# Two output projections of a graph and attention block, from one f32 matmul to three f32r matmuls

## The reference, cut to what matters

```
# layer 0, inside the mixing branch
out = transpose(out).reshape(B, N, DIM)
x = xn + (out @ proj_w + proj_b)              # xn: the normalised input of the branch
h = layernorm(x, ln2_g, ln2_b)                # goes to the MLP; x + xn rows are kept for the sum
# layer 1: the same product with W_proj, b_proj; the branch's result is
gamma * layernorm_core(xn + out @ W_proj + b_proj) + beta
```

## Time and profile before

| what | value |
|---|---|
| median of three runs | 3432.07 us (3430.57 to 3433.05) |
| profiled execution | 3428.94 us, of which the span is 3427.2 us |
| mean granted TensorE clock | 0.933 |
| PE busy | 2888.5 us, 84% of the span |
| DVE busy | 2312.9 us, 67% |
| ACT busy | 1449.7 us, 42% |
| GpSimd busy | 462.6 us, 13% |
| `proj0` (first load issued to next stage's first load) | 702.25 to 820.02 us |
| `proj1` (first load issued to next stage's first load) | 2771.16 to 2882.87 us |

### The profile page before, as it was taken

One profiled execution on the slowest core, in us unless ns is written; L12 is line 12 of the kernel. 1 busy time (PEld: TensorE's weight loads), 2 busy tenths in 40 slices (PEclk: granted clock), 3 DMA queues, 4 the chain that ended last, 5 costly groups with the idle time before them and its releaser, 6 DMA issues. The chain is left out here.

```text
span 3427.2 us, 50208 instructions
## 1 busy us (share of the span) xinstructions
PE 2888.5 (84%) x17656; PEld 2481.1 (72%) x17656; DVE 2312.9 (67%) x4167; ACT 1449.7 (42%) x2424; POOL 462.6 (13%) x327
## 2 busy tenths in 40 slices
PE   1999996967999998887988599868999977887794
PEld 1999995745788998777986233248999955777794
DVE  4665652735851553998664888657788858998775
ACT  3464552213112332555243577521546512554345
POOL 2287885200000000000002310000000000000000
PEclk9999998988999999999999699979999988999997
DMA  8333325694211653623131311253311077212301
GB/s 249 85 49 57 47 33 134 213 220 98 77 44 56 184 174 98 170 66 80 35 75 29 98 40 45 55 167 120 72 46 45 23 178 212 76 50 78 84 21 47
DMA packets 255535, 319.45 MB, mean 93 GB/s; under 512 B 97933, under 2 KB 179342, under 8 KB 255208
## 3 DMA queue, kind: packets, MB, share of 16 engines
q1 hardware_dynamic: 177576, 272.11, 29.4%
q0 software_dynamic: 77760, 44.83, 6.6%
HBM read 236.35 MB, written 79.53 MB: 92 GB/s over the span
## 5 line engine op out<-in xcount | busy, mean ns | idle before, releaser
L195 POOL DMA_INDIRECT adj_d<-edge_val,edge_off x160 | 332.5, 2078 | 184.6 <-DVE edge_off L183 100.0
L3191 DVE TENSOR_TENSOR expert_wgel<-expert_gel,expert_wps 128x417 f32<-128x417 f32 (+1 forms) x384 | 203.0, 584 | 57.0 <-PE expert_wps L3116 46.6
L2102 PE MATMUL gat00att_ops<-gat00att_h,gat00att_p 125*125 x1600 | 198.2, 280 | 48.4 <-DVE gat00att_p L2076 48.4
L2102 PE MATMUL gat10att_ops<-gat10att_h,gat10att_p 125*125 x1600 | 195.9, 279 | 48.4 <-DVE gat10att_p L2076 48.4
L2102 PEld LDWEIGHTS gat00att_ops<-gat00att_h,gat00att_p 125*125 125x125 f32 x1600 | 183.8, 189 | 63.0 <-issue 63.0
L2102 PEld LDWEIGHTS gat10att_ops<-gat10att_h,gat10att_p 125*125 125x125 f32 x1600 | 184.1, 192 | 60.8 <-issue 60.8
L3163 ACT ACTIVATE expert_gel<-expert_hps 128x417 f32<-128x417 f32 (+1 forms) x384 | 193.5, 519 | 64.2 <-DVE expert_wgel L3191 52.5
L577 PE MATMUL perf_wide<-y_lo,perf_qk_hi 128*128 128x416 f32 (+1 forms) x432 | 154.9, 359 | 24.7 <-DVE perf_qk_lo L759 24.4
L1275 PE MATMUL fc_ps<-y_lo,fc_w_hi 128*128 128x512 f32 (+1 forms) x432 | 154.6, 358 | 22.3 <-DVE fc_w_lo L1317 22.3
L1428 PE MATMUL fc_ops<-fc_w_hi,fc_x_lo 128*125 128x384 f32 x480 | 163.7, 341 | 7.1 <-DVE fc_w_lo L1480 7.1
L715 ACT ACTIVATE perf_kphi<-perf_wide,perf_lnm 125x384 f32<-125x384 f32 (+1 forms) x180 | 95.7, 630 | 172.5 <-PE perf_wide L601 171.6
(11 more groups left out here) (491 smaller groups left out, 7932.0 us busy)
## 6 DMA issues: line engine op xcount, KB each, us to landing
fc_w<-in_L_mix_fc_w SPq DMA_DIRECT2D x96, 384.0 KB
adj_d<-edge_zero POOLq DMA_DIRECT2D x22, 546.9 KB
gat00proj_adj<-adj_d POOLq DMA_DIRECT2D x20, 546.9 KB, 7.0
perf_keys<-keys_d SPq DMA_DIRECT2D x20, 437.5 KB
gat00att_sh<-shift_d SPq DMA_DIRECT2D x16, 546.9 KB
sh<-shift_d SPq DMA_DIRECT2D x16, 546.9 KB
perf_w<-in_L_mix_qkv_w SPq DMA_DIRECT2D x18, 384.0 KB
perf_w<-in_L_mix_W_qkv SPq DMA_DIRECT2D x18, 384.0 KB
```

The costliest lines, as they stand in the source:

```text
L195: edges.nc.gpsimd.indirect_dma_start(out=edges.adj_flat[u].rearrange("(n a) -> n a", a=1), out_offset=bass.IndirectOffsetOnAxis(ap=edges.o ...
L2102: ins = pe.matmul(ops[0:TP, u, b, t * w:(t + 1) * w], p[:, s, (t0 + t) * TP:(t0 + t + 1) * TP], h[:, s, bass.ds(hd, 1), :], start=(s == 0 ...
L3191: dve.tensor_tensor(wgel[:, q % W, 0:cn], gel[:, q % 3, 0:cn], wps[:, q % 3, 0:cn], ALU.mult).then_inc(wgel_done, 1)
```

## The change

Both projections are computed as three f32r matmuls for each f32 one. Weight and turned rows are each split into a high part (the value rounded to f32r) and a low part (what is left): ACT writes the high part, DVE subtracts it and writes the low part. PE then adds `hi x lo`, `lo x hi` and `hi x hi` for every block and half. The other parts of the change:

- `w` is loaded in 6 blocks of rows instead of 2 halves of columns, and `a` tile by tile with a semaphore each. `a` of tile 1 is now issued behind the whole of `w`. All else stays in its order, except that `a` of tiles 5 to 9 are five pairs of transfers.
- `w` lies in the space of `x` tiles 4 to 9 (`xw`), so SP waits until `w` is split before it issues `x` of tiles 2 to 4 and what follows.
- The loop over blocks is outside that over halves.
- The bias add (`base`) moves from DVE to GpSimd, as does in `proj1` the add of the shift rows to `x` (`shift_row`) and the one add of `more`. GpSimd does them in one list, in `proj1` base and shift in turn for each tile.
- `kept` now counts only the split tiles of `a`; the turned results of `proj0` have `y_kept`.

```diff
-        x = S.sb("x", [TP, NT, D])
-        w = S.sb("w", [128, KB, D])
-        aT = S.sb("aT", [128, 2, KB, TP])
+        xw = S.sb("xw", [128, NT, D])
+        x, w = xw[0:TP], xw[:, NT - KB:NT, :]
+        w_hi, w_lo = S.sb("w_hi", [128, KB, D], F32R), S.sb("w_lo", [128, KB, D], F32R)
+        aT_hi, aT_lo = S.sb("aT_hi", [128, 2, KB, TP], F32R), S.sb("aT_lo", [128, 2, KB, TP], F32R)
...
-                load_tiles(a, attn_d, a_ld, 0)
-                load_w(0)
-                load_w(1)
+                load_a(0)
+                for kb in range(KB):
+                    load_w(kb)
+                load_a(1)
                 move_rows(sp, bias[:], row_bcast(bias_d, TP), bias_ld)
...
+                load_tiles(h, xn_d, xn_ld, 1)
+                sp.wait_ge(w_split, KB)
+                load_tiles(x, x_d, x_ld, 1)
+                for t in range(5, NT):
+                    load_a(t)
+                load_tiles(h, xn_d, xn_ld, 2)
+                load_tiles(x, x_d, x_ld, 2)
...
+                    for kb in range(KB):
                         if t == 0:
-                            pe.wait_ge(w_ld[c], 16)
+                            pe.wait_ge(w_split, kb + 1)
+                        for c in range(2):
+                            for n, (ap, wp) in enumerate(((aT_hi, w_lo), (aT_lo, w_hi), (aT_hi, w_hi))):
+                                ins = pe.matmul(hps[0:TP, t % 2, c * 512:c * 512 + half], ap[:, t % 2, kb, :],
+                                                wp[:, kb, c * half:(c + 1) * half], start=(kb == 0 and n == 0),
+                                                stop=(kb == KB - 1 and n == 2))
...
+                    act.copy(aT_hi[:, t % 2], turned_a(t)).then_inc(a_high, 1)
+
+                def high_w(kb):
+                    act.wait_ge(w_ld[kb], 16)
+                    act.copy(w_hi[:, kb, :], w[:, kb, :]).then_inc(w_high, 1)
...
+                def base(t):
+                    if t in first_of:
+                        pool.wait_ge(xn_ld[first_of[t]], 32)
+                    pool.tensor_tensor(h[:, t, :], h[:, t, :], bias[:], ALU.add).then_inc(based, 1)
+                def shift_row(t):
+                    if t in first_of:
+                        pool.wait_ge(x_ld[first_of[t]], 32)
+                    pool.tensor_tensor(x[:, t, :], x[:, t, :], rows[0:TP, 1, :], ALU.add).then_inc(shifted, 1)
...
+                for t in range(2, NT):
+                    base(t)
+                    if not turn:
+                        shift_row(t)
...
+                def low_a(t):
+                    dve.wait_ge(a_high, t + 1)
+                    dve.tensor_tensor(aT_lo[:, t % 2], turned_a(t), aT_hi[:, t % 2].bitcast(F32), ALU.subtract).then_inc(kept, 1)
+
+                def low_w(kb):
+                    dve.wait_ge(w_high, kb + 1)
+                    dve.tensor_tensor(w_lo[:, kb, :], w[:, kb, :], w_hi[:, kb, :].bitcast(F32),
+                                      ALU.subtract).then_inc(w_split, 1)
...
+                low_a(0)
+                for kb in range(KB):
+                    low_w(kb)
                 for t in range(NT):
+                    if t + 1 < NT:
+                        low_a(t + 1)
                     project(t)
```

More of the change, by code:

```diff
@@ L994, in proj_stage @@
     first_of = {t0: p for p, (t0, _) in enumerate(pieces)}
+    half = D // 2
     turns = [("a", 0)]
@@ L1155, in _ @@
                         keep_y(t)
+            @block.gpsimd
+            def _(pool):
+                def base(t):
[6 more added lines that the diff above has]
+                    pool.tensor_tensor(x[:, t, :], x[:, t, :], rows[0:TP, 1, :], ALU.add).then_inc(shifted, 1)
+                pool.wait_ge(bias_ld, 32)
+                base(0)
+                base(1)
+                if not turn:
+                    pool.wait_ge(rows_ld, 96 if more is not None else 64)
+                    if more is not None:
+                        pool.tensor_tensor(rows[0:TP, 1, :], rows[0:TP, 1, :], more[:], ALU.add).then_inc(more_added, 1)
+                        pool.wait_ge(more_added, 1)
+                    shift_row(0)
+                    shift_row(1)
+                for t in range(2, NT):
+                    base(t)
+                    if not turn:
+                        shift_row(t)
             @block.vector
@@ L1163, in _ @@
                     shifts.keep(dve)
-                dve.wait_ge(bias_ld, 32)
+                def low_a(t):
[5 more added lines that the diff above has]
+                                      ALU.subtract).then_inc(w_split, 1)
                 def project(t):
-                    if t in first_of:
-                        dve.wait_ge(xn_ld[first_of[t]], 32)
-                    steps_done.done(dve.tensor_tensor(h[:, t, :], h[:, t, :], bias[:], ALU.add))
+                    dve.wait_ge(based, t + 1)
                     dve.wait_ge(h_done, t + 1)
-                    steps_done.wait()
                     both = h[:, t, :].rearrange("p (c n) -> p c n", c=2)
@@ L1181, in normalise @@
                 def normalise(t):
[L1182 to L1183 removed]
                     if turn:
+                        if t in first_of:
+                            dve.wait_ge(x_ld[first_of[t]], 32)
                         dve.tensor_tensor(x[:, t, :], x[:, t, :], h[:, t, :], ALU.add).then_inc(sum_ready, 1)
@@ L1195, in normalise @@
                         steps_done.done(dve.tensor_tensor(h[:, t, :], h[:, t, :], rows[0:TP, 0, :], ALU.mult))
-                        steps_done.done(dve.tensor_tensor(x[:, t, :], x[:, t, :], rows[0:TP, 1, :], ALU.add))
+                        dve.wait_ge(shifted, t + 1)
                         steps_done.wait()
@@ L1208, in _ @@
                         dve.wait_ge(rows_ld, 96 if more is not None else 64)
-                        if more is not None:
-                            steps_done.done(dve.tensor_tensor(rows[0:TP, 1, :], rows[0:TP, 1, :], more[:], ALU.add))
-                            steps_done.wait()
                     if t:
```

50 lines of the change are left out of this document (25 added, 25 removed).

## The result

Over the runs taken together the kernel before has a median of 3432.97 us (3430.57 to 3436.07, 8 runs) and the changed one 3415.43 (3406.62 to 3422.74, 8 runs): ratio 0.9948, interval 0.9936 to 0.996, so 14 to 22 us faster. The forecast was 3414. The profiled execution took 3415.68 us with a span of 3413.6; before it was 3427.2.

The account below looks back on a forecast made before the run. PE was taken to bound both projections, at 9.03 and 8.38 us a tile. Gains of 13.1 - 2 = 11.1 us in `proj0` and 10.9 - 4 = 6.9 in `proj1`, 18.0 together, gave 3414 from 3432.07; range 3402 to 3427.

Parts of the forecast that it names:

- The products: PE's tiles in both stages: f32r products take 6.96 us a tile in `proj1`, 7.61 in `proj0`, 1.42 less each.
- The head: Start of each stage: first product from 716.8 and 2785.5, second product ending 1.7 and 1.6 us earlier than before.
- later than 720: Sign against the forecast, at the head of `proj0`: a first product starting after 720 would show it wrong.
- The late `x`: GpSimd's list in `proj1`: `x` lands at about 2839, delaying tile 6's bias add and the last product by 5.3 us.
- what the sum had without exclusion: `proj1` before any price for GpSimd's adds: 16.2 us less 5.3 for the wait on `x`, 10.9 us gained.
- the 16.2 of the forecast: `proj1`: gain from PE and DVE taken alone, without the wait on `x` or a price for GpSimd's adds.
- DVE's tail: End of `proj1`: DVE's 9.5 us after the last product lose two shift adds of 0.95 each, leaving 7.6.
- The exclusion: GpSimd's adds beside DVE in both stages: they stop DVE steps, costing 2 us in `proj0` and 4 in `proj1`.
- in full: Rival: GpSimd's adds stop DVE for their whole length, 6 us in `proj0`, 11 in `proj1`; 3425 us; chance 0.20.
- No price: Rival: GpSimd's adds cost DVE nothing in either stage, gains 13.1 + 10.9 = 24.0 us; 3408 us; chance 0.22.
- so the gain is passed on whole: Stages behind start with a barrier and their own loads, so the two stages' 18.0 us shorten the whole kernel.

Follow-up runs that it names:

- e2: The changed kernel with GpSimd's bias and shift adds cut to one column each, order and waits kept: 3401.01 us.
- e9: The changed kernel with all adds back on DVE, `proj1`'s norm fused into two steps, and 101 empty DVE instructions in `proj0`: 3389.25 us.
- e3: The changed kernel with all bias adds of a piece ahead of its shift adds in GpSimd's list: 3414.28 us.
- e8: The changed kernel with 112 empty DVE instructions at the head of `proj0`: 3403.73 us.
- e11: The changed kernel with 40 empty DVE instructions ahead of the first subtraction in `proj0`: 3402.30 us.
- e7: The kernel before with 117 empty DVE instructions at the head of `proj0`: 3417.48 us.
- e12: The changed kernel with only the shift adds back on DVE, bias adds still on GpSimd, and 113 empty DVE instructions: 3403.95 us.

## Why the prediction was right, and where it was not

- **The products** went as said: 6.96 us a tile.
- **The head.** Forecast: first product from 14.5 us after the stage's start in `proj0`, done at 23.4. Measured: 721.11 - 706.6 = 14.5, taken up by DVE at 729.39 - 706.6 = 22.8. In `proj1` DVE took it up at 2784.49, 23.1 after the start, and 23.2 was the forecast. The absolute test ("later than 720") was badly put: the stage began 4.3 us later.
- **The late `x`.** The forecast had it at 2839, 67.8 us after the stage's start; GpSimd took it up 66.7 after. Product 8 waited 3.46 us, at the place named; an earlier wait of 2.49, ahead of product 4, was not named. In `e2`, with the waits and without wide adds, `proj1` gave 10.9 us, just what the sum had without exclusion. But the term was sized at 5.3, and PE's waits for the low part in `e2` add up to 2.9 us. In `e9`, where GpSimd stands idle, the last matmul of the stage begins 87.2 us after its start, in `e2` 90.0, so the late `x` was worth about 3. That puts `proj1` without it at a gain of some 13.7 us (an estimate, 10.9 + 2.8) and not at the 16.2 of the forecast. One part of the difference is DVE's tail up to the next stage's first load, which became 1.3 us shorter and not 1.9. Two errors of some 2.5 us cancelled, and that is luck.
- **The exclusion.** Against the stages of `e2` those of the changed kernel are 1.1 us longer in `proj0` (2 taken) and 5.0 in `proj1` (4 taken); in the other f32r kernels with both sets of adds (`e3`, `e8`, `e11`) it is 6.2 to 6.5 in `proj1`. DVE's blocked steps in `proj1` add up to 14.9 us, as the two groups shown and the tensor_scalar (9.8, 0.68 each alone) give: 17.2 - 9.6 + 12.0 - 7.7 + 9.8 - 6.8. Slack took the larger part, about 10 us. The rival "in full" (11 us) is refuted by the stage's length, though the blocked time is even more than it said. "No price" is refuted by the rows. (The DVE step of 2.92 us in the earlier trace rows, which the forecast calls an add, is a multiplication; it has two SBUF inputs all the same.)
- **Added when they overlap.** In the changed kernel DVE was 0.88 us early for the late bias add, not 3.76 as in `e2`: it had been stopped before. The two terms share their time; that their sum was near is partly chance.
- **The step without a ground** is "so the gain is passed on whole". By the medians it held: 17.5 us against the stages' 17.3. But `e7` shows that the stages outside can move the time by 15 us through DVE's instruction count alone, and no term of the forecast had a place for it. The total came right because the loop stalls at 2182 and at 2187 alike (263.7 and 263.5 us). A begin at 2227, 40 instructions further, gave 13 us more (`e11`).

## What to carry to other kernels

An add moved from DVE to GpSimd is paid for in DVE's steps with two SBUF inputs and in its scalar and cast passes beside it: compare what it frees with what it stops, and try first to fold DVE's own steps. Where a program has a runtime loop of some hundred instructions, as the 294 here, a change of code ahead of it can add or take its stall; look for idle time released by "issue" at the loop's turns, and compare variants at the same place of the loop.

## What had not been expected

- Idle time of 2.6 to 2.9 us at each jump back of a DVE loop, set by where its 294 instructions begin. With the fall of TensorE's clock that follows most of them it is 10 to 11 us in the loop, more than half of this change's whole effect.
- In `proj0` GpSimd's adds stop a cast (2.18 us instead of 0.55) and a tensor_scalar with one SBUF input (2.01 instead of 0.68), but never an add with a PSUM operand (0.96 us at most in all fourteen traces):

```profile
769.78 2.01 DVE L1246 TENSOR_SCALAR proj_a<-proj_h,proj_mv,proj_rstd 125x768 f32<-125x768 f32 x1
771.72 2.18 DVE L112 CAST y_hi<-proj_full 128x750 fp32r<-128x750 f32 x1
```
- What a row of GpSimd adds costs depends on where in DVE's turn it begins. `proj0` was 3.8 us longer in `e8`, with its 112 empty DVE instructions (96 ns each, between 708.24 and 718.96 us), and 2.6 us longer in `e12`, with 113. In `e8` the empty instructions did not delay the head: DVE took up the first product 22.8 us after the stage's start in both. The loss comes where GpSimd's five adds in a row (from 762.91 on, 10.29 us) meet DVE, which then is at its tensor_scalar, its cast and the subtraction behind it:

```profile
763.08 2.09 DVE L1250 TENSOR_SCALAR proj_a<-proj_h,proj_mv,proj_rstd 125x768 f32<-125x768 f32 x1
765.09 2.18 DVE L112 CAST y_hi<-proj_full 128x750 fp32r<-128x750 f32 x1
767.30 2.43 DVE L114 TENSOR_TENSOR y_lo<-proj_full,y_hi 128x750 fp32r<-128x750 f32 x1
```

  In the changed kernel the same subtraction had its 0.94 us. DVE took up the product of tile 5 at 62.3 us after the stage's start in `e8` and at 59.2 in the changed kernel. `e12` has it at 62.4. So the exclusion cost `proj0` 1.1 us in one kernel and 4.8 in another; the forecast had taken 2, out of 0 to 6. With all adds on DVE, 101 empty instructions cost the stage at most 0.6 us.
